# Splitting the two wide tiles of each attention diagonal into high and low parts, the low part made by VectorE

## The chip, the cores and the metric

The kernel runs on one core of a Trainium2 chip. Its time is in device microseconds (us). An execution gives one time; the profiled execution also gives the span from the first to the last instruction of the program.

## The reference, cut to what matters

The model is a feed-forward part (512 to 4096 to 512, 4-bit weights), causal attention, and the same feed-forward part again, each with a layer norm and a residual, on 2048 tokens of 512 features in fp32. The change is in attention:

```python
q, k, v = split(x_norm @ w_qkv.T + b_qkv)        # 16 heads of 32 features, 2048 tokens
scores = einsum('bhqd,bhkd->bhqk', q, k) / sqrt(32)
scores = scores + causal                          # -inf above the diagonal
out = einsum('bhqk,bhkd->bhqd', softmax(scores), v)
```

## The kernel before

Stages run one after the other: feed-forward, projections, `attention`, output projection, feed-forward. This change touches `attention` alone.

Within `attention` the queries of a head stand in 4 blocks of 512. Block b needs the key tiles 0 to 4b+3, 128 keys each, so a head has 4+8+12+16 = 40 tiles, called slots 0 to 39 here (`TILES`). In a block the key tiles 4b to 4b+3 lie on the diagonal and are 512, 384, 256 and 128 queries wide; all others are 512 wide. Block 0 has its diagonal tiles in slots 0, 1, 2, 3 (widest first). In the later blocks every b full tiles are followed by one diagonal tile, narrowest first, so the tiles of 384 and 512 queries stand in slots 9 and 11, 20 and 23, 35 and 39.

A product in full fp32 reads its operands as they are. A split product uses a high part (fp32r, rounded) and a low part (what the rounding left) and takes two matmuls in fp32r. Before the change the tiles below the diagonal (24 a head, `SPLIT`) have split probabilities, and the 16 diagonal tiles (`WHOLE`) plain fp32 ones.

Each engine works through its own instructions in the order written. For slot t they are:

- TensorE (PE), in `head`: the scores of slot t+4 (L1211, and L1215 for the mask on the diagonal), one chunk of scores of the next head for its row maxima (L699, L703), at slots 4, 12, 23 and 39 the "rows" (L712, four small transposes that bring the negated maxima of block 0, 1, 2 or 3 of the next head into the rows of its queries), then slot t's probabilities times the values: L1228 for a whole tile, L1231 and L1234 for high and low of a split one.
- ScalarE (ACT): the exponentials of slot t+4 from a score bank, L1283 for `probs`, and L1285 for `probs_high` of a split tile; rows back into `queries` (L742) at the slots of the rows; the block's output out of PSUM (L1292).
- GpSimd (POOL): `probs_low` = `probs` minus `probs_high` for the split tiles, one after the other (L1324).
- VectorE (DVE): the maximum of each chunk (L721). After the chunks of slots 2, 10, 21 and 37 it makes the block's maxima ready for the rows, with `split_max`: a reduction (L729), a CAST to fp32r (L734), and a subtraction of 4 columns (L736), the last of which lets the rows go.

What ties them: three score banks (the scores of slot t+4 wait for the exponentials of slot t+1), a ring of 5 slots for the probabilities, three banks for chunks and rows. The heads are 5 passes of a hardware loop over three heads, and the last head by itself, in which there is no next head, so no chunks, no maxima and no rows.

Of the kernel before, what the change touches and what calls it, by code (L numbers as in the profile page):

```python
# [16 lines left out]
P = 128  # L17
# [3 lines left out]
TB = 512  # L21
# [27 lines left out]
def f32(ap):  # L49

    return ap.bitcast(F32)
# [532 lines left out]
AHEAD = 4  # L584
RING = AHEAD + 1

WHOLE = [t for t in range(SLOTS) if TILES[t][1] >= 4 * TILES[t][0]]
SPLIT = [t for t in range(SLOTS) if t not in WHOLE]


def chunks_of_slot(t):

    return [m for m in range(SLOTS) if m * (SLOTS - 2) // SLOTS == t]
# [533 lines left out]
def attention(nc, bank, o_parts, sums, inverses, w_out, b_out, heads, o):  # L1127
    with ExitStack() as ctx:
# [3 lines left out]
        def sem(name):  # L1132
            return ctx.enter_context(nc.semaphore(name))
# [12 lines left out]
        scores_ready = sem("scores_ready")  # L1146
        probs_ready = sem("probs_ready")
        probs_low_ready = sem("probs_low_ready")
        out_ready = sem("out_ready")
        out_free = sem("out_free")  # L1150
        out_stored = [sem(f"out_stored{i}") for i in range(2)]
# [43 lines left out]
        @block.tensor  # L1195
        def _(pe):

            def scores(hp, s, t, first=False):

                b, kt = TILES[t]  # L1200
                i = s % 3
                if t in FIRST_OF_BLOCK:
                    pe.wait_ge(heads.rows_ready, 12 * hp + (4 * s + b + 1))
                    if s == 2 and b == 0:
                        pe.wait_ge(heads.constants_ready, 10)
                if not (first and t < SCORE_BANKS):
                    pe.wait_ge(probs_ready, 120 * hp + (SLOTS * s + t - SCORE_BANKS + 1))
                q0 = max(b * TB, kt * P)
                width = (b + 1) * TB - q0
                out = score_bank[(SLOTS * s + t) % SCORE_BANKS]  # L1210
                last = pe.matmul(out[:, 0:width], keys[i][0:ROWS, cols(kt, P)],  # L1211
                                 queries[i][0:ROWS, q0:q0 + width], start=True, stop=(kt < 4 * b),
                                 skip_group_check=True)
                if kt >= 4 * b:
                    last = pe.matmul(out[:, 0:P], heads.ident_b[:], heads.key_mask_b[:],  # L1215
                                     start=False, stop=True, skip_group_check=True)
                last.then_inc(scores_ready, 1)

            def with_values(hp, s, t):
                b, kt = TILES[t]  # L1220
                i = s % 3
                if t in FIRST_OF_BLOCK:
                    pe.wait_ge(out_free, 12 * hp + (4 * s + b + 1))
                pe.wait_ge(probs_ready, 120 * hp + (SLOTS * s + t + 1))
                off = max(0, kt * P - b * TB)
                out = out_bank[b % 2][0:VCOLS, off:TB]
                if t in WHOLE:
                    last = pe.matmul(out, f32(values[i][:, kt, :]), probs[:, t % RING, 0:TB - off],  # L1228
                                     start=(t in FIRST_OF_BLOCK), stop=(t in LAST_OF_BLOCK), skip_group_check=True)
                else:  # L1230
                    pe.matmul(out, values[i][:, kt, :], probs_high[:, t % RING, 0:TB - off],  # L1231
                              start=(t in FIRST_OF_BLOCK), stop=False, skip_group_check=True)
                    pe.wait_ge(probs_low_ready, 3 * len(SPLIT) * hp + (len(SPLIT) * s + SPLIT.index(t) + 1))
                    last = pe.matmul(out, values[i][:, kt, :], probs_low[:, t % RING, 0:TB - off],  # L1234
                                     start=False, stop=(t in LAST_OF_BLOCK), skip_group_check=True)
                if t in LAST_OF_BLOCK:
                    last.then_inc(out_ready, 1)

            def head(hp, s, has_next):
                for t in range(SLOTS):  # L1240
                    if t + AHEAD < SLOTS:
                        scores(hp, s, t + AHEAD)
                    elif has_next:
                        scores(hp, s + 1, t + AHEAD - SLOTS)
                    if has_next:
                        for m in chunks_of_slot(t):
                            heads.max_chunk(pe, hp, s + 1, m)
                        if t in ROWS_AT:
                            heads.rows(pe, hp, s + 1, ROWS_AT[t])
                    with_values(hp, s, t)  # L1250

            for t in range(AHEAD):
                scores(0, 0, t, first=True)
            with pe.Fori(0, HEADS // 3) as hp:
                for s in range(3):
                    head(hp, s, True)
            head(HEADS // 3, 0, False)

        @block.vector
        def _(dve):  # L1260
            def head(hp, s):
                for t in range(SLOTS):
                    for m in chunks_of_slot(t):
                        heads.take_max(dve, hp, s + 1, m)
                    if t in MAXED_AT:
                        heads.split_max(dve, hp, s + 1, MAXED_AT[t])

            heads.fill_ones(dve, 2)
            with dve.Fori(0, HEADS // 3) as hp:
                for s in range(3):  # L1270
                    head(hp, s)
            dve.wait_ge(o.sums_loaded, 16)
            early, _ = o.inverse_tile(EARLY_HEADS)
            dve.reciprocal(early, early).then_inc(o.inverse_ready, 1)

        @block.scalar
        def _(act):
            def exps(hp, s, t):
                b, kt = TILES[t]
                width = TB - max(0, kt * P - b * TB)  # L1280
                act.wait_ge(scores_ready, 120 * hp + (SLOTS * s + t + 1))
                source = score_bank[(SLOTS * s + t) % SCORE_BANKS][:, 0:width]
                last = act.activation(probs[:, t % RING, 0:width], source, ACT.Exp, scale=SM_SCALE)  # L1283
                if t in SPLIT:
                    last = act.activation(probs_high[:, t % RING, 0:width], source, ACT.Exp, scale=SM_SCALE)  # L1285
                last.then_inc(probs_ready, 1)

# [28 lines left out]
        @block.gpsimd  # L1316
        def _(pool):
            def low(hp, s, t):
                if t in WHOLE:
                    return  # L1320
                b, kt = TILES[t]
                width = TB - max(0, kt * P - b * TB)
                pool.wait_ge(probs_ready, 120 * hp + (SLOTS * s + t + 1))
                pool.tensor_tensor(probs_low[:, t % RING, 0:width], probs[:, t % RING, 0:width],  # L1324
                                   f32(probs_high[:, t % RING, 0:width]), ALU.subtract)\
                    .then_inc(probs_low_ready, 1)

            def head(hp, s):
                for t in range(SLOTS):
                    low(hp, s, t)  # L1330
# [235 lines left out]
```

## Time and profile before

| what | us |
|---|---|
| median of 3 runs (lowest, highest) | 3196.67 (3193.45, 3202.14) |
| the profiled execution: its time | 3196.54 |
| its span | 3194.7 |
| attention, from 1299 to 2008 us of the span | 709 |
| of it the last head | 40 |
| PE busy in those 709 us | 654.93 |
| ACT busy | 556.77 |
| POOL busy | 485.25 |
| DVE busy | 444.19 |

The busy time of PE is from modelled ends of pipelined matmuls, so the work of a matmul is better read from the distance between two starts. The times below are of one execution. The inner heads repeat: the same slot takes the same time in each but for a few hundredths of a us.

### The profile page before, as it was taken

The numbers are of one execution on the slowest core, as the hardware profiler recorded it, in microseconds if no ns is written. First come the engines' busy times: TensorE is split into PE (matmuls) and PEld (weight loads), VectorE is DVE, ScalarE is ACT, GpSimd is POOL, SyncE is SP. The second block draws the span as 40 slices with busy tenths as digits, with TensorE's granted clock in tenths as the row PEclk, the third lists the DMA queues.
The fourth block names the chain that finished last, engine by engine and source line by source line (L and its number), as shares of the span: only waits on it lengthen the run. The fifth ranks groups of instructions, "written<-read, shape, count | busy, mean of one in ns | idle before, by whom it ended". The sixth has DMA issues, their size and how long they took to land. (4 is left out here: it accounts for less than half of the span.)

```text
span 3194.7 us, 40306 instructions
## 1 busy us (share of the span) xinstructions
PE 3015.3 (94%) x13408; PEld 2316.5 (73%) x13408; DVE 1945.8 (61%) x2795; ACT 1263.3 (40%) x2213; POOL 1264.9 (40%) x880
## 2 busy tenths in 40 slices
PE   5999999999999989999999999669999999999999
PEld 3788888888888758555555555447888888888887
DVE  7666656665666465666666664476666566665664
ACT  4322222222222242677777778233222222222222
POOL 4322222222222175566666767433222222222221
PEclk9999999999999989999999999789999999999999
DMA  2000000000000039322222240310000000000001
GB/s 92 21 27 27 26 20 26 26 26 20 20 26 14 28 93 253 105 47 66 65 64 49 54 105 23 114 40 20 27 27 26 20 23 23 26 26 20 26 13 53
DMA packets 123898, 144.37 MB, mean 45 GB/s; under 512 B 71904, under 2 KB 72160, under 8 KB 120480
## 3 DMA queue, kind: packets, MB, share of 16 engines
q1 hardware_dynamic: 123256, 142.70, 15.8%
q8 instruction: 42, 0.69, 0.1%
q10 hardware_dynamic: 552, 0.59, 0.1%
q14 instruction: 48, 0.39, 0.0%
HBM read 105.26 MB, written 38.01 MB: 45 GB/s over the span
## 5 line engine op out<-in xcount | busy, mean ns | idle before, releaser
L60 PE MATMUL psum<-ffn_x_high,ffn_w_high 128*128 128x512 f32 x2048 | 803.3, 392 | 17.2 <-DVE ffn_gelu L388 17.2
L525 POOL TENSOR_TENSOR ffn_inner<-ffn_gelu,ffn_inner 128x512 fp32r<-128x512 f32 x256 | 346.2, 1352 | 1156.4 <-ACT ffn_inner L470 1156.4
L61 PE MATMUL psum<-ffn_x_low,ffn_w_high 128*128 128x512 f32 x2048 | 798.9, 390 | 0.0
L62 PE MATMUL psum<-ffn_x_high,ffn_w_low 128*128 128x512 f32 x2048 | 798.6, 390 | 0.0
L1324 POOL TENSOR_TENSOR probs_low<-probs,probs_high 128x512 fp32r<-128x512 f32 x384 | 483.5, 1282 | 223.7 <-ACT probs_high L1285 223.2
L378 DVE SCALAR_TENSOR_TENSOR ffn_gelu<-ffn_gelu,psum 128x512 f32<-128x512 f32 x256 | 176.0, 688 | 599.1 <-ACT ffn_gelu L463 599.0
L721 DVE TENSOR_REDUCE chunk_max<-psum 128x1 f32<-128x512 f32 (+3 forms) x640 | 383.4, 610 | 217.2 <-PE psum L699 113.0
L60 PEld LDWEIGHTS psum<-ffn_x_high,ffn_w_high 128*128 128x128 f32 x2048 | 386.2, 189 | 103.0 <-DVE ffn_gelu L388 20.9
L61 PEld LDWEIGHTS psum<-ffn_x_low,ffn_w_high 128*128 128x128 f32 x2048 | 386.0, 188 | 81.6 <-issue 2.0
L62 PEld LDWEIGHTS psum<-ffn_x_high,ffn_w_low 128*128 128x128 f32 x2048 | 385.7, 188 | 80.5
L60 PE MATMUL psum<-ffn_inner,ffn_w_high 128*128 128x512 f32 x1024 | 398.6, 389 | 0.2
L61 PE MATMUL psum<-ffn_inner,ffn_w_high 128*128 128x512 f32 x1024 | 398.4, 389 | 0.0
L62 PE MATMUL psum<-ffn_inner,ffn_w_low 128*128 128x512 f32 x1024 | 398.4, 389 | 0.0
L1283 ACT ACTIVATE probs<-psum 128x512 f32<-128x512 f32 (+3 forms) x640 | 341.4, 548 | 96.6 <-PE psum L1211 57.3
L463 ACT ACTIVATE ffn_gelu<-psum 128x512 f32<-128x512 f32 x256 | 152.8, 597 | 530.9 <-PE psum L62 530.9
L519 POOL TENSOR_TENSOR ffn_w_low<-ffn_weight,ffn_w_high 128x1024 fp32r<-128x1024 f32 x96 | 232.1, 2418 | 329.5 <-ACT ffn_w_high L456 329.5
L394 DVE SCALAR_TENSOR_TENSOR x<-psum,x 128x512 f32<-128x512 f32 x512 | 321.3, 683 | 16.0 <-PE psum L62 16.0
L470 ACT ACTIVATE ffn_inner<-ffn_gelu 128x512 fp32r<-128x512 f32 x256 | 161.9, 632 | 381.2 <-DVE ffn_gelu L388 381.2
L1211 PE MATMUL psum<-queries,keys 98*128 98x512 f32 (+3 forms) x640 | 298.5, 467 | 3.0 <-ACT probs_high L1285 2.1
L382 DVE SCALAR_TENSOR_TENSOR ffn_gelu<-ffn_gelu,psum 128x512 f32<-128x512 f32 x256 | 176.2, 688 | 180.0 <-ACT ffn_gelu L465 180.0
L456 ACT ACTIVATE ffn_w_high<-ffn_weight 128x1024 fp32r<-128x1024 f32 x96 | 102.0, 1062 | 398.9 <-DVE ffn_weight L369 398.9
L699 PE MATMUL psum<-keys,queries 96*128 96x512 f32 (+3 forms) x640 | 248.9, 398 | 1.0 <-DVE chunk_max L721 0.7
(124 smaller groups left out, 3989.3 us busy)
## 6 DMA issues: line engine op xcount, KB each, us to landing
ffn_words<-packed SPq DMA_DIRECT2D x96, 256.0 KB
ffn_word_scales<-scales SPq DMA_DIRECT2D x96, 256.0 KB
qk_parts<-parts SPq DMA_DIRECT2D x32, 512.0 KB, 4.4
queries<-qk_parts SPq DMA_DIRECT2D x48, 256.0 KB, 4.6
keys<-qk_parts SPq DMA_DIRECT2D x48, 256.0 KB, 6.6
v_parts<-parts SPq DMA_DIRECT2D x16, 512.0 KB, 6.1
values<-v_parts SPq DMA_DIRECT2D x16, 512.0 KB, 10.9
o_parts<-heads_out SPq DMA_DIRECT2D x64, 128.0 KB
```

Source lines behind the costliest of these rows:

```text
L60: pe.matmul(out, w_high, x_high, start=first, stop=False, skip_group_check=True)
L61: pe.matmul(out, w_high, x_low, start=False, stop=False, skip_group_check=True)
L62: return pe.matmul(out, w_low, x_high, start=False, stop=last, skip_group_check=True)
L382: dve.scalar_tensor_tensor(out=cubic[m], in0=square[m], scalar=1.0, in1=gate_bank[m], op0=ALU.add, op1=ALU.mult)\
L394: dve.scalar_tensor_tensor(out=x[:, k, cols(tb, TB)], in0=down_bank[k], scalar=FFN_BACK, in1=x[:, k, cols(tb, TB)], op0=ALU.mult, op1=ALU. ...
L519: pool.tensor_tensor(w_low[s][:, :, piece, :], weight[:, q % 2, :, :], f32(w_high[s][:, :, piece, :]), ALU.subtract).then_inc(w_low_ready, 1)
L525: pool.tensor_tensor(inner[:, tb % 2, m, 1, :], product[m], f32(inner[:, tb % 2, m, 0, :]), ALU.subtract)\
L699: last = pe.matmul(out[:, 0:width], self.queries[i][0:self.STACK, cols(qt, P)], self.keys[i][0:self.STACK, c * TB:c * TB + width], start=T ...
L721: dve.tensor_reduce(self.chunk_max[:, b % 2, qt % 4, c:c + 1], self.max_bank[max_bank_of(s, ("chunk", m))][:, 0:width], AX.X, ALU.max).the ...
L1211: last = pe.matmul(out[:, 0:width], keys[i][0:ROWS, cols(kt, P)], queries[i][0:ROWS, q0:q0 + width], start=True, stop=(kt < 4 * b), skip_g ...
L1283: last = act.activation(probs[:, t % RING, 0:width], source, ACT.Exp, scale=SM_SCALE)
L1324: pool.tensor_tensor(probs_low[:, t % RING, 0:width], probs[:, t % RING, 0:width], f32(probs_high[:, t % RING, 0:width]), ALU.subtract)\
```

## The change

The diagonal tiles of 512 and 384 queries (`WIDE`, 8 a head) get the same treatment as the tiles below the diagonal: ACT makes a second exponential into `probs_high`, PE makes two fp32r matmuls in place of one in fp32. Their low part is made by DVE, not by POOL, in `wide_low`, two slots ahead of the slot in which PE needs it, and has a semaphore of its own. The two narrow diagonal tiles (256 and 128 queries) stay plain fp32. POOL's list of work stays as it was. In the last head DVE, which had nothing to do there, gets the low parts of its wide tiles.

```diff
-WHOLE = [t for t in range(SLOTS) if TILES[t][1] >= 4 * TILES[t][0]]
-SPLIT = [t for t in range(SLOTS) if t not in WHOLE]
+WHOLE = [t for t in range(SLOTS) if TILES[t][1] >= 4 * TILES[t][0] + 2]
+WIDE = [t for t in range(SLOTS) if 0 <= TILES[t][1] - 4 * TILES[t][0] < 2]
+SPLIT = [t for t in range(SLOTS) if t not in WHOLE and t not in WIDE]
+WIDE_AHEAD = 2
...
-                    pe.wait_ge(probs_low_ready, 3 * len(SPLIT) * hp + (len(SPLIT) * s + SPLIT.index(t) + 1))
+                    if t in WIDE:
+                        pe.wait_ge(wide_low_ready, 3 * len(WIDE) * hp + (len(WIDE) * s + WIDE.index(t) + 1))
+                    else:
+                        pe.wait_ge(probs_low_ready, 3 * len(SPLIT) * hp + (len(SPLIT) * s + SPLIT.index(t) + 1))
...
+            def wide_low(hp, s, t):
+                if t not in WIDE:
+                    return
+                b, kt = TILES[t]
+                width = TB - (kt * P - b * TB)
+                dve.wait_ge(probs_ready, 120 * hp + (SLOTS * s + t + 1))
+                dve.tensor_tensor(probs_low[:, t % RING, 0:width], probs[:, t % RING, 0:width],
+                                  f32(probs_high[:, t % RING, 0:width]), ALU.subtract).then_inc(wide_low_ready, 1)
...
+            def head(hp, s, has_next):
                 for t in range(SLOTS):
-                    for m in chunks_of_slot(t):
-                        heads.take_max(dve, hp, s + 1, m)
-                    if t in MAXED_AT:
-                        heads.split_max(dve, hp, s + 1, MAXED_AT[t])
+                    if t + WIDE_AHEAD < SLOTS:
+                        wide_low(hp, s, t + WIDE_AHEAD)
+                    elif has_next:
+                        wide_low(hp, s + 1, t + WIDE_AHEAD - SLOTS)
+                    if has_next:
+                        for m in chunks_of_slot(t):
+                            heads.take_max(dve, hp, s + 1, m)
+                        if t in MAXED_AT:
+                            heads.split_max(dve, hp, s + 1, MAXED_AT[t])
...
-                if t in SPLIT:
+                if t not in WHOLE:
                     last = act.activation(probs_high[:, t % RING, 0:width], source, ACT.Exp, scale=SM_SCALE)
...
             def low(hp, s, t):
-                if t in WHOLE:
+                if t not in SPLIT:
                     return
```

DVE's queue of the kernel before, around slot 21 of a head: the chunk maxima (TENSOR_REDUCE of `chunk_max`) of slots 20 and 21, and the maxima of block 2 made ready for the rows.

```order
L721 TENSOR_REDUCE chunk_max<-psum 128x1
L719 REGISTER_ALU
L721 TENSOR_REDUCE chunk_max<-psum 128x1
L729 TENSOR_REDUCE minus_max<-chunk_max 128x4
L731 REGISTER_ALU
L733 REGISTER_ALU
L734 CAST max_parts<-minus_max 128x4
```

The same place of DVE's queue after the change, where the lines of the code stand three further down:

```order
L724 TENSOR_REDUCE chunk_max<-psum 128x1
L1273 REGISTER_ALU
L1274 TENSOR_TENSOR probs_low<-probs,probs_high 128x512
L722 REGISTER_ALU
L724 TENSOR_REDUCE chunk_max<-psum 128x1
L732 TENSOR_REDUCE minus_max<-chunk_max 128x4
L734 REGISTER_ALU
L736 REGISTER_ALU
L737 CAST max_parts<-minus_max 128x4
```

The low part of slot 23 (512 queries) now stands between the maximum of slot 20's chunk and that of slot 21's, ahead of the three steps that the rows of block 2 wait for. At slot 37 the low part of slot 39 stands in the same way ahead of block 3's, and the low parts of slots 9 and 11 ahead of the maxima of slots 7 and 9.

PE's queue before, around slot 23: a chunk of the next head, the rows of block 2, slot 23's product with the values, and the scores of slot 28.

```order
L699 MATMUL psum<-keys,queries 128x512
L709 REGISTER_ALU
L686 REGISTER_ALU
L712 MATMUL psum<-ident_r,max_parts 2x128 x4
L1228 MATMUL psum<-probs,values 65x512
L1207 REGISTER_ALU
L1211 MATMUL psum<-queries,keys 128x512
```

PE's queue after, at the same place:

```order
L702 MATMUL psum<-keys,queries 128x512
L712 REGISTER_ALU
L689 REGISTER_ALU
L715 MATMUL psum<-ident_r,max_parts 2x128 x4
L1235 MATMUL psum<-probs_high,values 65x512
L1238 REGISTER_ALU
L1241 MATMUL psum<-probs_low,values 65x512
L1211 REGISTER_ALU
L1215 MATMUL psum<-queries,keys 128x512
```

Nothing of PE's order has moved: two matmuls stand where one stood, and between them is a wait for DVE.

## Rows read from the trace of the kernel before

**Rows 1.** Windows of attention; busy us and instructions of each engine, clock, DMA.

```profile
1299.00:2008.00 709.00, 654.93 (x3256) 402.87 (x3256) 444.19 (x783) 556.77 (x1150) 485.25 (x387) 0.98 0.26 62
```

**Rows 2.** Waits in attention: who waited for whom, total us, times, longest.

```profile
PE psum L712 <- DVE max_parts L736: 48.6, 45, 1.9
```

**Rows 3.** Timeline of PE, slots 10 to 12: start us, us, what, [idle before].

```profile
1538.05 0.40 PE L1211 MATMUL psum<-queries,keys 98*128 98x512 f32 x1
1538.28 0.40 PE L699 MATMUL psum<-keys,queries 96*128 96x512 f32 x1
1538.51 1.02 PE L1228 MATMUL psum<-probs,values 128*65 128x512 f32 x2
...
1539.61 0.39 PE L699 MATMUL psum<-keys,queries 96*128 96x512 f32 x1
```

**Rows 4.** Timeline of ACT, slots 19 to 21, then two of its pauses before.

```profile
1543.72 0.61 ACT L1285 ACTIVATE probs_high<-psum 128x512 fp32r<-128x512 f32 x1
1544.20 0.99 ACT L1283 ACTIVATE probs<-psum 128x384 f32<-128x384 f32 x2
1545.05 0.63 ACT L1285 ACTIVATE probs_high<-psum 128x512 fp32r<-128x512 f32 x1
...
1535.46 0.60 ACT L1283 ACTIVATE probs<-psum 128x512 f32<-128x512 f32 x1 [0.33 <-PE psum L1211]
1538.48 0.60 ACT L1283 ACTIVATE probs<-psum 128x512 f32<-128x512 f32 x1 [0.78 <-PE psum L1211]
```

**Rows 5.** Timeline of DVE and POOL in the output projection: both read SBUF.

```profile
2014.21 0.69 DVE L1424 TENSOR_TENSOR from_high<-from_high,from_low 128x512 f32<-128x512 f32 x1 [41.95 <-PEq L1128]
2016.37 3.40 POOL L1474 TENSOR_TENSOR normed_low<-from_high,normed_high 128x512 fp32r<-128x512 f32 x2 [5.61 <-ACT normed_high L1467]
2016.88 1.76 DVE L1424 TENSOR_TENSOR from_high<-from_high,from_low 128x512 f32<-128x512 f32 x1
```

**Rows 6.** Timeline of DVE and POOL around the rows of block 1.

```profile
1538.79 0.37 DVE L734 CAST max_parts<-minus_max 128x4 fp32r<-128x4 f32 x1
...
1536.62 2.51 POOL L1324 TENSOR_TENSOR probs_low<-probs,probs_high 128x512 fp32r<-128x512 f32 x2 [0.62 <-ACT probs_high L1285]
1539.64 2.62 POOL L1324 TENSOR_TENSOR probs_low<-probs,probs_high 128x512 fp32r<-128x512 f32 x2 [0.50 <-ACT probs_high L1285]
```

**Rows 7.** Timeline of all engines around the rows of block 2.

```profile
1548.75 3.75 POOL L1324 TENSOR_TENSOR probs_low<-probs,probs_high 128x512 fp32r<-128x512 f32 x3 [0.28 <-ACT probs_high L1285]
...
1546.59 1.93 DVE L721 TENSOR_REDUCE chunk_max<-psum 128x1 f32<-128x384 f32 x3 [0.38 <-PE psum L703]
1549.01 0.69 DVE L721 TENSOR_REDUCE chunk_max<-psum 128x1 f32<-128x512 f32 x1 [0.49 <-PE psum L703]
...
1550.03 1.28 DVE L734 CAST max_parts<-minus_max 128x4 fp32r<-128x4 f32 x1
...
1551.34 1.18 DVE L736 TENSOR_TENSOR max_parts<-minus_max,max_parts 128x4 fp32r<-128x4 f32 x1
...
1552.65 0.40 PE L712 MATMUL psum<-ident_r,max_parts 128*2 128x128 f32 x4 [1.86 <-DVE max_parts L736]
```

**Rows 8.** Timelines of POOL, DVE and PE around the rows of block 3.

```profile
1561.76 5.02 POOL L1324 TENSOR_TENSOR probs_low<-probs,probs_high 128x512 fp32r<-128x512 f32 x4
...
1566.77 0.69 DVE L721 TENSOR_REDUCE chunk_max<-psum 128x1 f32<-128x512 f32 x1 [0.38 <-PE psum L703]
...
1568.28 0.40 PE L712 MATMUL psum<-ident_r,max_parts 128*2 128x128 f32 x4 [0.27 <-DVE max_parts L736]
```

**Rows 9.** Timeline of POOL in the last head.

```profile
1981.40 24.89 POOL L1324 TENSOR_TENSOR probs_low<-probs,probs_high 128x512 fp32r<-128x512 f32 x20 [0.17 <-ACT probs_high L1285]
```

**Rows 10.** Timelines behind a loop's turn, and a window (columns as in rows 1).

```profile
1572.15 0.60 ACT L1283 ACTIVATE probs<-psum 128x512 f32<-128x512 f32 x1 [1.98 <-PE psum L1215]
1575.96 0.59 PE L712 MATMUL psum<-ident_r,max_parts 128*2 128x128 f32 x4 [1.34 <-DVE max_parts L736]
...
1575.00:1582.00 7.00, 6.04 (x27) 4.01 (x28) 3.88 (x7) 4.68 (x10) 3.32 (x3) 0.76 1.10 217
```

More of the change, by code:

```diff
@@ L1148, in attention @@
         probs_low_ready = sem("probs_low_ready")
+        wide_low_ready = sem("wide_low_ready")
         out_ready = sem("out_ready")
@@ L1260, in _ @@
         def _(dve):
-            def head(hp, s):
-                for t in range(SLOTS):
-                    for m in chunks_of_slot(t):
-                        heads.take_max(dve, hp, s + 1, m)
-                    if t in MAXED_AT:
-                        heads.split_max(dve, hp, s + 1, MAXED_AT[t])
+            def wide_low(hp, s, t):
[7 more added lines that the diff above has]
+            def head(hp, s, has_next):
+                for t in range(SLOTS):
+                    if t + WIDE_AHEAD < SLOTS:
[7 more added lines that the diff above has]
+                            heads.split_max(dve, hp, s + 1, MAXED_AT[t])
             heads.fill_ones(dve, 2)
+            for t in range(WIDE_AHEAD):
+                wide_low(0, 0, t)
             with dve.Fori(0, HEADS // 3) as hp:
                 for s in range(3):
-                    head(hp, s)
+                    head(hp, s, True)
             dve.wait_ge(o.sums_loaded, 16)
@@ L1274, in _ @@
             dve.reciprocal(early, early).then_inc(o.inverse_ready, 1)
+            head(HEADS // 3, 0, False)
         @block.scalar
```

## The prediction

> **What bounds the kernel now.** The windows say where to look: in attention PE is busy 654.93 of 709 us, ACT 557, POOL 485, DVE 444 [rows 1]. PE sets the pace. What it loses goes mostly to one wait, the rows' wait for DVE's last step of the maxima: 48.6 us in 45 waits, of 60 rows, four a head in 15 heads [rows 2]. The timelines say why. The rows of block 2 idle 1.86 us and those of block 3 0.27 us [rows 7, 8]; 48.6 over 15 heads is 3.24 a head, so 1.1 are left for block 0, if those of block 1 (the fourth that 45 of 60 leaves out) have none.
>
> DVE's CAST on 4 columns takes 0.37 us at one place and 1.28 at another [rows 6, 7], and at 1550.03 to 1552.52 both the CAST and the subtraction end just where two of POOL's three subtractions end (1548.75 plus 1.25 for each gives 1550.00, 1551.25 and 1552.50). So DVE's instructions that take two operands or two ports from SBUF wait while POOL runs, and POOL takes over again between the CAST and the subtraction. With large tiles the two alternate: a subtraction of 512 columns is 0.69 us alone, and 1.76 us when it starts 0.5 us into POOL's; POOL's two took 3.40 us, not 2.5 [rows 5]. I read the 0.9 as two waits, for a DVE instruction that ran when POOL came and for the one at 2016.88 that got in between. So a DVE low part costs DVE 0.60 us between neighbours and the POOL instruction behind it 0.44 us, 384 columns three quarters of that.
>
> **PE's part.** The fp32 product of 512 columns: from its start at 1538.51 to the next L699 at 1539.61 is 1.10 us; of that 0.23 is the one scores' matmul between them (as from 1538.05 to 1538.28), so it costs 0.87 us. Two fp32r ones cost 0.46. Saved: 0.40. At 384 columns three quarters: 0.29 [rows 3]. Four of each a head are 2.76 us, over 15 heads 41.4 us. This is the gain if nothing else moves.
>
> **ACT's part.** A second exponential is 0.48 us at 512 columns (1543.72 to 1544.20), and 0.37 at 384 (0.85 for a 384 and a 512, from 1544.20 to 1545.05) [rows 4]. That is 3.4 us a head; with 16 heads ACT goes from 557 to 611 us and stays below PE. Where it stands ahead of a due slot it eats pauses: between slots 9 and 15 it gets 0.85 us more work and had pauses of 0.33 and 0.78 us [rows 4]. It just fits.
>
> **The rows, one after the other.** Here the gain is kept or lost, so I carry the sum through a head. Times are those of before plus the shift.
>
> Block 0 (slot 4). PE is 0.69 us earlier (slots 0, 1). Slot 2's maximum and the exponential that POOL's next subtraction waits for both hang on PE, so all move together and the wait of 1.1 us stays [rows 2]. Shift -0.69.
>
> Block 1 (slot 12). Slots 9 and 11 bring PE there 1.38 us early, at 1538.46 (0.23 behind the last row of [rows 3] is 1539.84). DVE reaches its CAST 0.98 us earlier, as slot 9's saving counts there but not slot 11's, at 1537.81 [rows 6]. POOL does not follow: its pair began at 1536.62, behind ACT. ACT's added 0.85 us leave slot 12's high part 0.3 us earlier, not 0.98, so POOL's pair starts at 1536.31 and goes to 1538.83. Then slot 15's subtraction is ready (its exponential moves by 0.98 with its scores, from 1538.48 to 1537.50, and the second ends 1.08 later, at 1538.58) and follows at once. The CAST is held to 1538.86 and the small subtraction, free before, is held until 1540.10. The rows go at 1540.23: a new wait of 1.77 us. Shift -1.38 + 1.77 = +0.39.
>
> Block 2 (slot 23). Slot 20 saves 0.29: +0.10. `wide_low` of slot 23 stands ahead of the last chunk's maximum. Its probabilities are there by 1547.9: ACT reaches slot 21's second exponential at 1545.05 plus 0.37 for slot 20, and has then four of 0.48, the last complete 0.60 after its start [rows 4]. DVE's chunks before it ended at 1548.52, now some 0.35 later, so it is free at 1548.85, and POOL pauses there (0.28 us before 1548.75) [rows 7], now until 1549.1, as slot 24's exponentials move with PE, by up to 0.39. DVE gets in first, to 1549.43; POOL's next subtraction ends at 1550.6. The maximum of the last chunk, taken at 1549.01 before, is taken at 1549.45, the CAST comes 1.02 us behind its start as before, at 1550.46, waits 0.15 us and not 0.95, and the small subtraction waits for one whole subtraction of POOL, to 1551.87. The rows go at 1552.0, not 1552.65. The wait falls from 1.86 to 1.11 us. Shift +0.10 - 0.75 = -0.65, and -1.05 behind slot 23's product.
>
> Block 3 (slot 39). POOL is nearly the bound here: four subtractions without a pause end at 1566.78 [rows 8]. Slot 35's low part costs it 0.33 us. Shifted, its last one runs from 1564.8 to 1566.05. DVE comes to slot 39's low part at 1565.0, ahead of the last chunk's maximum, and is held to 1566.05, done at 1566.58. The maximum (0.69) and the three small steps unhindered (0.82, as from 1567.46 to 1568.28 before) bring the rows to 1568.0. PE was ready at 1568.01 (1568.28 less 0.27), is now at 1566.67 (1.05 + 0.29 earlier), and waits 1.33 us. Shift -0.28, and -0.66 behind slot 39's product, rounded.
>
> **The sum.** The low parts of slots 0 and 1 come when DVE has no chunk. So a head gives -2.76 + 1.77 - 0.75 + 1.06, that is -0.66 us: 15 heads -9.9. In the four heads behind a turn of the loop ACT idles 1.98 us, and DVE's CAST meets POOL's first subtraction; there PE waits 1.34 us [rows 10]. DVE comes 0.69 earlier and passes before POOL starts: 0.65 us more each, -2.6. The last head is bound by POOL: 20 subtractions without a pause in 24.89 us [rows 9]. Four low parts get between them (two of 0.44, two of 0.33), ACT's 0.85 ahead of them delay their start, and the last product saves 0.40: +2.0. Together -10.5 us. The profiled execution took 3196.54 (its span 3194.7), 0.1 from the median, so the forecast is 3186.0.
>
> **The clock.** After the wait at 1575.96 the granted clock is 0.76 over 7 us [rows 10], so TensorE went part of the time at 1.2 of its 2.4 GHz, behind the idle time. That is 1.7 us lost (0.24 of 7). In attention the clock is 0.98 [rows 1], so 709 times 0.02, some 14 us, of such stretches. The change removes four such waits and adds others (slots 12, 39). I take no change; bounds are 7 us either way.
>
> **A page that speaks against it.** The Trainium skill (SBUF — State Buffer, "SBUF: two separate sides") says that VectorE and GpSimd share a port pair under an exclusive lock, held for the whole instruction, and that a VectorE instruction with two SBUF inputs needs it. The trace agrees: 1.76 us beside 0.69 [rows 5]. By that rule the times of the two engines add up on the pair. In numbers of this case: POOL's 485 us and 64 low parts, half of 0.60 and half of 0.45 us (67 us), are 552 of some 700 us. So the pair is no bound on the average, and what it costs is where one instruction stands behind another, as in the walk above.
>
> **Rivals.**
>
> A. The waits stay as they are, and all of PE's 41.4 us show, less the last head's 2.0: 3157. For it: DVE is idle 265 of 709 us. Against it: the walk above puts four low parts into POOL's way. Chance 0.10.
>
> B. Slower: DVE comes too late to slot 23's low part, after POOL has begun slot 24's. The margin is 0.25 us (1548.85 against 1549.1); and it rests on times that I carried over twenty slots. Then the low part ends at 1550.95, and the last maximum, CAST and small subtraction follow with two more subtractions of POOL between: rows at 1553.5, 1.5 us later than forecast, in 15 heads +22: 3208. It decides as soon as DVE is 0.25 us later there, for then DVE waits for the whole of POOL's instruction. Chance 0.22.
>
> C. The small subtraction at block 1 slips in before POOL. It needs slot 15's high part 0.25 us later than 1538.58, or POOL's pair earlier by as much; then one subtraction less, 1.25 us in 15 heads, -19: 3167. Chance 0.20.
>
> D. Nothing moves, because what PE saves, each row gives back: 3197. Chance 0.05.
>
> The forecast itself has 0.43. Its own bounds: a clock of 7 us either way, and 0.3 us a head for the price of POOL's delay (0.3 to 0.7 us a low part): 3176 to 3198.
>
> **The numbers.** Under A and C it is faster; so is the forecast in some 45 of 100 of its cases, since 0.3%, what a measurement of this kernel tells from no change, is 9.6 us and the forecast stands at 10.5. Faster 0.49, same 0.28, slower 0.23. The range leaves A out below and the upper half of B above: 3163 to 3210.
>
> **What the profile of the changed kernel would show.** PE's two matmuls for slot 23 0.46 us, no fp32 product of 512 columns left. Four rows a head with waits of 1.1, 1.8, 1.1, 1.3 us: the wait of PE for DVE's last small step grows from 48.6 us to about 73. DVE's low parts of 0.6 us where POOL rests and 1.0 to 1.8 where it doesn't. In the last head POOL's 20 subtractions end about 2.4 us later. If the rows of block 1 go without a wait, C holds; if those of block 2 wait about 2.8 us, B does. The prediction is wrong if ACT turns out to hold PE back (its waits for exponentials are short now), or if POOL and DVE don't take turns as in the output projection.

## The result: slower, 3227.1 us against 3197.0

| | before | changed |
|---|---|---|
| median, us | 3197.01 (6 runs, 3192.85 to 3202.14) | 3227.06 (6 runs, 3200.16 to 3234.43) |
| ratio | 1 | 1.0075, 95% interval 1.0044 to 1.0105 |
| profiled execution, us (span) | 3196.54 (3194.7) | 3202.68 (3200.9) |

The forecast was 3186.0, its range 3163 to 3210. The six times of the changed kernel fall into two groups: 3200.16 and 3202.68, and four from 3225.72 to 3234.43. The profile is of the run of 3202.68, one of the two low ones, so what it shows is the smaller part of the loss; the first experiment shows the larger. "DVE's low part" below is the subtraction that DVE makes for a wide tile (line 1274).

The page of the changed kernel, two lines of it, and the window of its attention (columns as in [rows 1]):

```profile
span 3200.9 us, 40712 instructions
...
PE 2974.4 (93%) x13408; PEld 2315.1 (72%) x13408; DVE 2055.4 (64%) x2923; ACT 1306.0 (41%) x2341; POOL 1274.5 (40%) x880
```
```profile
1299.00:2014.00 715.00, 618.10 (x3260) 403.04 (x3260) 553.70 (x914) 600.59 (x1279) 497.19 (x388) 0.97 0.26 62
```

PE's busy time in attention fell from 654.93 us [rows 1] to 618.10, as the change means it to. DVE's rose by 109.5 us where the forecast's low parts were 67. From its first scores to its last product attention takes 708.7 us before and 711.3 after. That is 2.6 of the 6.2 us by which the two spans differ; the other 3.6 fall outside attention (2.2 ahead of it, 1.4 behind it), where the code is the same, and are taken as spread between executions.

The waits in attention (who waited for whom, total us, times, longest) answer to [rows 2]:

```profile
PE psum L715 <- DVE max_parts L739: 73.5, 56, 2.2
...
PE psum L1241 <- DVE probs_low L1274: 12.9, 3, 7.6
```

The first line is the rows' wait, 48.6 us before, and "about 73" was forecast. The second was not forecast: three times PE waited for a low part of DVE's.

**What went as forecast.** The timelines of PE, then of DVE and POOL, around the rows of block 1 (line 715 is the old 712, 1235 and 1241 multiply the high and the low part, 737 is the CAST, 739 the small subtraction):

```profile
1630.96 0.39 PE L1235 MATMUL psum<-probs_high,values 128*65 128x512 f32 x1
1631.18 0.39 PE L1241 MATMUL psum<-probs_low,values 128*65 128x512 f32 x1
...
1633.63 0.40 PE L715 MATMUL psum<-ident_r,max_parts 128*2 128x128 f32 x4 [1.57 <-DVE max_parts L739]
```
```profile
1631.23 1.06 DVE L737 CAST max_parts<-minus_max 128x4 fp32r<-128x4 f32 x1
1632.32 1.18 DVE L739 TENSOR_TENSOR max_parts<-minus_max,max_parts 128x4 fp32r<-128x4 f32 x1
...
1629.72 5.00 POOL L1348 TENSOR_TENSOR probs_low<-probs,probs_high 128x512 fp32r<-128x512 f32 x4 [0.65 <-ACT probs_high L1309]
```

The second product starts 0.23 us behind the first, and the next matmul 0.23 behind the second (0.46 together, where the prediction reads 0.87 from [rows 3] for the fp32 one). The CAST, 0.37 us in [rows 6], takes 1.06, the small subtraction 1.18: POOL's four subtractions now stand together, and both steps of DVE's end where one of them ends (near 1632.3 and 1633.5). The rows wait 1.57 where they had waited for nothing. Blocks 2 and 3 of the same head:

```profile
1642.27 0.68 DVE L1274 TENSOR_TENSOR probs_low<-probs,probs_high 128x512 fp32r<-128x512 f32 x1
...
1643.87 0.26 DVE L737 CAST max_parts<-minus_max 128x4 fp32r<-128x4 f32 x1
1644.16 1.18 DVE L739 TENSOR_TENSOR max_parts<-minus_max,max_parts 128x4 fp32r<-128x4 f32 x1
...
1645.47 0.40 PE L715 MATMUL psum<-ident_r,max_parts 128*2 128x128 f32 x4 [1.14 <-DVE max_parts L739]
...
1654.62 1.29 DVE L1274 TENSOR_TENSOR probs_low<-probs,probs_high 128x384 fp32r<-128x384 f32 x1
...
1658.53 1.57 DVE L1274 TENSOR_TENSOR probs_low<-probs,probs_high 128x512 fp32r<-128x512 f32 x1
...
1661.53 0.40 PE L715 MATMUL psum<-ident_r,max_parts 128*2 128x128 f32 x4 [1.32 <-DVE max_parts L739]
```

Slot 23's low part comes in a pause of POOL's of 0.46 us (and takes 0.68 us) and the rows of block 2 wait 1.14, not the 1.86 of [rows 7]. Slot 35's takes 1.29 and slot 39's 1.57, each behind one subtraction of POOL, and the rows of block 3 wait 1.32, not the 0.27 of [rows 8].

**What did not.** DVE, POOL and PE at slot 35 in the first head, and then DVE at slot 35 in the second head:

```profile
1340.89 0.69 DVE L724 TENSOR_REDUCE chunk_max<-psum 128x1 f32<-128x512 f32 x1 [0.21 <-PE psum L702]
1341.49 5.04 DVE L1274 TENSOR_TENSOR probs_low<-probs,probs_high 128x384 fp32r<-128x384 f32 x1
1346.46 2.53 DVE L724 TENSOR_REDUCE chunk_max<-psum 128x1 f32<-128x384 f32 x4
...
1337.39 8.73 POOL L1348 TENSOR_TENSOR probs_low<-probs,probs_high 128x512 fp32r<-128x512 f32 x7
...
1343.64 0.34 PE L1235 MATMUL psum<-probs_high,values 128*65 128x384 f32 x1
1346.59 0.58 PE L1241 MATMUL psum<-probs_low,values 128*65 128x384 f32 x1 [2.62 <-DVE probs_low L1274]
```
```profile
1387.22 0.69 DVE L724 TENSOR_REDUCE chunk_max<-psum 128x1 f32<-128x512 f32 x1 [0.22 <-PE psum L702]
1387.83 1.29 DVE L1274 TENSOR_TENSOR probs_low<-probs,probs_high 128x384 fp32r<-128x384 f32 x1
```

The same instruction with the same neighbours takes 5.04 us in one head and 1.29 in the next. The row of POOL's shows the last seven of eight subtractions without a pause (from 1336.15 on). The seven take 8.73 us, 1.247 each, so no DVE instruction got between any of them: they change at 1342.38, 1343.63 and 1344.87, all while DVE waits, and end at 1346.12. DVE is done at 1346.53, 0.41 us after POOL stopped of itself: behind slot 35 it had slots 36, 37 and 38 to do, and the next ones are DVE's (39) or on the next head's diagonal. This is called a miss from here on: DVE did not get in at a change of POOL's instruction, and then not at the next ones either. PE waited 2.62 us for it. The last head, DVE, POOL and PE:

```profile
1997.78 11.20 DVE L1274 TENSOR_TENSOR probs_low<-probs,probs_high 128x384 fp32r<-128x384 f32 x2 [9.06 <-ACT probs_high L1309]
...
1996.03 7.47 POOL L1348 TENSOR_TENSOR probs_low<-probs,probs_high 128x512 fp32r<-128x512 f32 x6
2003.43 4.52 POOL L1365 TENSOR_TENSOR wo_low<-wo,wo_high 128x2048 fp32r<-128x2048 f32 x1
...
2008.42 0.58 PE L1241 MATMUL psum<-probs_low,values 128*65 128x384 f32 x1 [7.63 <-DVE probs_low L1274]
```

Here DVE asks at 1997.78 and is let in at 2007.95, when `wo_low`, whose work has nothing to do with this head, is through as well. (POOL's row shows the last six of 20 subtractions without a pause.) All 128 low parts together (the view of one line: duration in ns, least, median, most):

```profile
L1274 DVE TENSOR_TENSOR probs_low<-probs,probs_high x128: 546/684/10596, 1303.5 to 2008.3; 128x512 fp32r<-128x512 f32 x64, 128x384 fp32r<-128x384 f32 x64
```

Only three of them are above 1.7 us, all of slot 35: 5.04 and 5.03 in the first and third head and 10.60 in the last.

### The profile page after: what moved, and what is told of

It reads as the page before. It is cut to its first block and busy times, and to the rows that moved or that the text cites. A ratio compares the mean times of both kernels' runs of the same rounds, so it can differ in the third digit from the quotient of the medians.

```text
span 3200.9 us, 40712 instructions
## 1 busy us (share of the span) xinstructions
PE 2974.4 (93%) x13408; PEld 2315.1 (72%) x13408; DVE 2055.4 (64%) x2923; ACT 1306.0 (41%) x2341; POOL 1274.5 (40%) x880
## 5 line engine op out<-in xcount | busy, mean ns | idle before, releaser
L1348 POOL TENSOR_TENSOR probs_low<-probs,probs_high 128x512 fp32r<-128x512 f32 x384 | 492.6, 1307 | 209.7 <-ACT probs_high L1309 208.7
L1307 ACT ACTIVATE probs<-psum 128x512 f32<-128x512 f32 (+3 forms) x640 | 361.6, 573 | 39.1 <-PE psum L1215 20.4
L1309 ACT ACTIVATE probs_high<-psum 128x512 fp32r<-128x512 f32 (+1 forms) x512 | 324.5, 634 | 0.0
L1215 PE MATMUL psum<-queries,keys 98*128 98x512 f32 (+3 forms) x640 | 254.9, 399 | 7.1 <-ACT probs_high L1309 6.2
```

## The experiments

In each, the ratio is to the kernel before, run beside it on the same chip: its median was 3195.09 for experiments 1 to 4, 3194.54 for 5 to 8 and 3194.97 for 9 and 10. The theory under test: what the change costs beyond the forecast is misses at slot 35. The rivals: it costs what the new waits of the rows cost, or POOL's being slowed, or ACT's added exponentials.

**1. The changed kernel again.** No edit, for a second profile.

> The changed kernel once more, for its spread and for a second profile. Theory S (starving): DVE's low part of slot 35 comes while POOL's subtractions follow one another without a pause, and gets in either at the first change between two of them or at none until POOL rests; each miss makes PE wait some 3 us, 8 us in the last head. Then the times fall in two groups, about 3200 and 3225 to 3235 us, and the slower a profile is, the more of slot 35's 16 low parts take 5 us or more (3 of 16 in the first profile; about 10 in a run of 3228). Theory C (clock): the slower executions have the same 3 misses and more stretches at 1.2 GHz behind the waits of the rows.

Measured: 3233.86 (3225.95 to 3234.84), ratio 1.0115 (1.0099 to 1.0130). The profile is of a run of 3233.04, one of the high group. Its waits and its low parts:

```profile
PE psum L715 <- DVE max_parts L739: 62.8, 49, 2.2
...
PE psum L1241 <- DVE probs_low L1274: 39.2, 13, 7.6
```
```profile
1431.45 5.07 DVE L1274 TENSOR_TENSOR probs_low<-probs,probs_high 128x384 fp32r<-128x384 f32 x1
```

13 of 16 low parts of slot 35 missed (twelve of 4.97 to 5.07 us, 10.60 in the last head) where the other profile has 3. The spans are 3231.2 and 3200.9, so 10 misses more go with 30.3 us more: 3.0 us each. They can be taken apart. PE waits 26.3 us more for line 1274 and 10.7 less for the rows (behind a miss the rows of block 3 mostly find their maxima ready); that is 15.6. The other half goes with the clock. The window of attention (columns as in [rows 1]):

```profile
1299.00:2045.00 746.00, 632.58 (x3260) 408.16 (x3260) 579.06 (x913) 603.32 (x1279) 493.44 (x388) 0.95 0.25 59
```

PE is busy 632.58 us with the same 3260 matmuls that took it 618.10 in the other profile, 14.5 more, and the granted clock is 0.95 against 0.97. Where the clock falls, two windows of the first profile's missed first head show:

```profile
1341.00:1346.00 5.00, 2.98 (x15) 1.63 (x13) 5.00 (x2) 3.83 (x8) 5.00 (x5) 1.00 0.00 0
1346.00:1350.00 4.00, 3.41 (x11) 1.88 (x11) 3.49 (x6) 1.48 (x4) 0.12 (x1) 0.57 0.00 0
```

PE is busy 2.98 of 5 us, and right behind that the granted clock is 0.57, most of the time the 1.2 GHz level. Not every miss is followed by this: behind the one at 1431.45 in the second profile the clock stays at 1.00. In these two profiles, then, the kernel's two speeds are few misses and nearly always a miss; the other eight runs of it have no profile.

**2. Slot 35 stays plain fp32.**

```diff
-WHOLE = [t for t in range(SLOTS) if TILES[t][1] >= 4 * TILES[t][0] + 2]
-WIDE = [t for t in range(SLOTS) if 0 <= TILES[t][1] - 4 * TILES[t][0] < 2]
+WIDE = [0, 1, 9, 11, 20, 23, 39]
+WHOLE = [t for t in range(SLOTS) if TILES[t][1] >= 4 * TILES[t][0] and t not in WIDE]
```

> Slot 35 (384 queries, block 3) stays plain fp32, the seven other wide tiles are split as in the change. Theory S: no low part meets four POOL subtractions in a row in the middle of block 3, no run is slow: all within 6 us, median 3185 to 3192 (the last head's wait of 8 us and those of 3 us gone, 0.29 us a head of PE's gain lost). Theory C: the waits of the rows stay and with them the clock's stretches, so the times still spread to 3225 and more.

Measured: 3183.21 (3181.14 to 3185.85), ratio 0.9966 (0.9952 to 0.9979), 2 us below the expected range. Without this one low part of eight the change is 12 us faster than before, and 50.7 us faster than with it (experiment 1); the rows' waits at blocks 1 and 2 are still there. One miss is left, in the last head, at slot 39 (6.76 us):

```profile
L1274 DVE TENSOR_TENSOR probs_low<-probs,probs_high x112: 549/683/6758, 1299.9 to 1983.0; 128x512 fp32r<-128x512 f32 x64, 128x384 fp32r<-128x384 f32 x48
```

**3. No low part by DVE at all.**

```diff
-                    if t in WIDE:
-                        pe.wait_ge(wide_low_ready, 3 * len(WIDE) * hp + (len(WIDE) * s + WIDE.index(t) + 1))
-                    else:
+                    if t not in WIDE:
                         pe.wait_ge(probs_low_ready, 3 * len(SPLIT) * hp + (len(SPLIT) * s + SPLIT.index(t) + 1))
-                    last = pe.matmul(out, values[i][:, kt, :], probs_low[:, t % RING, 0:TB - off],
+                    second = probs_high if t in WIDE else probs_low
+                    last = pe.matmul(out, values[i][:, kt, :], second[:, t % RING, 0:TB - off],
...
             def wide_low(hp, s, t):
-                if t not in WIDE:
-                    return
+                return
```

> The low part of the wide tiles is left out: DVE makes none, and PE's second matmul for such a tile reads the high part again, so PE and ACT have the work of the change and DVE and POOL that of before. Theory S, and the walk of the prediction: PE's 41 us show nearly whole, as the rows wait about as before: 3155 to 3168. Rival theory A (ACT's added exponentials hold PE back, not the port): 3185 or more.

This kernel leaves the low parts of the wide tiles out: PE's second product takes the high part once more, so its numbers are not the model's, and only its time is of use.

Measured: 3154.56 (3152.13 to 3156.65), ratio 0.9870 (0.9855 to 0.9886), 0.4 us below the expected range. ACT still makes its 128 added exponentials and PE its two products each, so ACT is not what makes the changed kernel slow. It also takes the rows' waits apart: 1.01, 1.6, 0.93 and 0.28 us at blocks 0 to 3 (0 and 0.99 at blocks 0 and 1 behind a loop's turn).

```profile
PE psum L715 <- DVE max_parts L739: 52.7, 57, 1.8
```

Block 1's new wait of 1.6 us comes without any low part of DVE's, from PE's earlier arrival and POOL's later pair, as the forecast derived it. Block 3's is the low parts' (0.28 without them).

**4. Low parts at slots 0, 1, 20 and 23 alone** (`WIDE = [0, 1, 20, 23]`, WHOLE as in 2).

> Only slots 0, 1, 20 and 23 of a head are split with DVE's low part; 9, 11, 35 and 39 stay plain fp32. By the walk of the prediction slots 9 and 11 bring a wait of 1.6 us ahead of the rows of block 1 for 0.69 us of PE, and 35 and 39 one of 1.0 us for as much; without them a head gives 0.69 + 0.29 + 0.40 and 0.7 us less wait at the rows of block 2, about 2.1 us: 3165, within 3160 to 3175, without slow runs. Theory C expects no better than 3190.

Measured: 3157.77 (3156.30 to 3158.71), ratio 0.9882 (0.9867 to 0.9897), below the expected range. The rows of block 1 don't wait, those of block 2 wait 1.35 us, those of block 3 0.28. A head takes 41.72 us instead of 43.6: twice 0.69 saved, 0.5 less wait at block 2, 1.88 together. That is 28 us in 15 heads. The rest goes with the clock: in the kernel before, seven of the 14 periods from one head's rows of block 2 to the next have a granted clock of 0.96 and are 1.5 to 2.5 us longer than 43.6, 14 us together, and here all 14 have 1.00. Four of the eight tiles bring nearly all that can be had.

**5. Slot 35 alone** (`WIDE = [35]`).

> Slot 35 alone is split with DVE's low part; the other seven stay plain fp32 as before. Theory S: PE gains 0.29 us a head (-4 us in all), each of the 16 low parts takes either 1.3 us or, when it is missed at every change of POOL, about 5; each miss costs 3 us, that of the last head 7. So 3198 us if only the last is missed, about 3240 if nearly all are. A rival theory, that the cost comes from the eight low parts together (DVE's load), expects 3190 to 3196 and no low part over 2 us.

Measured: 3225.19 (3217.18 to 3233.33), ratio 1.0105 (1.0086 to 1.0124). It lies within the expected 3198 to 3240. A single low part a head makes the kernel about as slow as all eight do.

```profile
L1274 DVE TENSOR_TENSOR probs_low<-probs,probs_high x16: 767/1293/10510, 1341.1 to 2012.0; 128x384 fp32r<-128x384 f32 x16
```

The profiled run is the lowest of its four (3217.18) and has four misses (4.7, 5.05, 5.05 and 10.51 us). Its attention is 18.9 us longer than that of before. In the kernel with this one tile a head without a miss takes 43.3 us at a clock of 1.00, 0.3 less than before, -4 us in 14 periods; the three periods with a miss are 5.1, 3.9 and 4.0 us above 43.3, with a clock of 0.93 and twice 0.96; and from the last rows of block 2 to the end it takes 9.6 us more. That adds up to 18.4; the periods at a low clock without a miss cost about as much as before (15 and 14 us).

**6. The changed kernel, and POOL made to yield once.** POOL waits, before its subtraction of slot 36, until slot 35's low part is done:

```diff
+                if t == 36:
+                    pool.wait_ge(wide_low_ready, 3 * len(WIDE) * hp + (len(WIDE) * s + WIDE.index(35) + 1))
```

> The changed kernel with one wait more: POOL starts slot 36's subtraction only when DVE's low part of slot 35 is done, so DVE gets the port at the latest there. The work is the same. Theory S: no low part of slot 35 over about 2 us, the last head's neither, the two groups of times become one: 3184 to 3192. The rival, that POOL must not be held up in block 3, expects each head longer by the wait: 3205 or more.

Measured: 3181.87 (3178.89 to 3185.16), ratio 0.9959 (0.9946 to 0.9973). All of the computation of the changed kernel is here, one wait is added, and the time is 45 us under the changed kernel's median (and 2 us below the expected range).

```profile
L1274 DVE TENSOR_TENSOR probs_low<-probs,probs_high x128: 549/684/2439, 1301.8 to 1987.4; 128x512 fp32r<-128x512 f32 x64, 128x384 fp32r<-128x384 f32 x64
```
```profile
1299.00:1992.00 693.00, 609.89 (x3256) 395.32 (x3256) 536.29 (x911) 598.52 (x1279) 493.66 (x388) 0.99 0.27 64
```

No low part is above 2.44 us, PE waits for none, and attention takes 692.3 us at a clock of 0.99. In all 15 inner heads POOL pauses 0.50 us ahead of slot 36, and DVE takes 1.29 to 1.35 us. The 2.44 us are of the last head: there DVE was passed over at one change of POOL's, and got in at the next, where POOL waits for it:

```profile
1983.38 2.44 DVE L1274 TENSOR_TENSOR probs_low<-probs,probs_high 128x384 fp32r<-128x384 f32 x1 [9.07 <-ACT probs_high L1309]
...
1973.83 11.58 POOL L1350 TENSOR_TENSOR probs_low<-probs,probs_high 128x512 fp32r<-128x512 f32 x9
1985.97 4.19 POOL L1350 TENSOR_TENSOR probs_low<-probs,probs_high 128x512 fp32r<-128x512 f32 x3 [0.56 <-DVE probs_low L1274]
```

The rows still wait (1.0, 1.6, 1.14 and, two heads of three, 1.34 us: 68.0 us in 51), so these waits are not what made the kernel slow. With experiments 2 and 5 this settles the cause.

**7. The maxima before the low part.** In each slot DVE first takes its chunk's maximum and the small steps and then makes the low part of the slot two ahead:

```diff
-                    if t + WIDE_AHEAD < SLOTS:
-                        wide_low(hp, s, t + WIDE_AHEAD)
...
                         if t in MAXED_AT:
                             heads.split_max(dve, hp, s + 1, MAXED_AT[t])
+                    if t + WIDE_AHEAD < SLOTS:
+                        wide_low(hp, s, t + WIDE_AHEAD)
```

> In DVE's order of each slot the chunk maxima and the steps for the rows come first and the low part two slots ahead comes behind them. By the walk of the prediction the rows of block 3 wait 0.3 us and not 1.3, and PE waits 0.1 to 0.4 us for slot 39's low part in its place; the wait of block 1's rows (1.6 us) stays, as it comes from ACT and POOL. Slot 35's low part still meets POOL without a pause, so misses of 5 us are still there and set the time: 3190 with few, 3225 with many. If the low parts' place ahead of the maxima were the cause of the loss, the time would be 3180 without any change at slot 35.

Measured: 3238.97 (3232.78 to 3245.42), ratio 1.0137 (1.0118 to 1.0155), 14 us above the 3225 expected with many misses.

```profile
PE psum L715 <- DVE max_parts L739: 52.0, 48, 2.2
...
PE psum L1241 <- DVE probs_low L1274: 41.8, 15, 7.6
```

The rows of block 3 wait 0.3 us or nothing, so the rival "the rows' waits" would have this faster. Instead it is slower than the changed kernel: slot 35's low part, asked for about 1 us later, takes 4.0 to 4.1 us in 14 of 15 heads and 10.6 in the last. Asking later makes a held low part shorter by as much and does not prevent the miss. The granted clock of attention is 0.94 here.

**8. Slots 9 and 11 alone** (`WIDE = [9, 11]`).

> Slots 9 and 11 alone are split with DVE's low part. By the walk of the prediction PE gains 0.69 us a head ahead of the rows of block 1, ACT's two added exponentials keep POOL where it was, and the rows wait 1.6 to 1.8 us in place of none: 0.9 us a head longer, so 3205 to 3212 us. If the gain of PE were kept there, 3185.

Measured: 3215.39 (3209.82 to 3219.05), ratio 1.0060 (1.0044 to 1.0075), 3 us above the expected range.

```profile
PE psum L715 <- DVE max_parts L739: 74.2, 61, 1.9
```

There are no misses (no low part above 0.91 us). The rows of block 1 wait 1.54 to 1.62 us in all 15 heads, and a head takes 44.7 us instead of 43.6: 0.69 saved and 1.58 lost is 0.9 of these 1.1. This pair is a loss by itself, which the sum of the forecast contained (-0.69 + 1.77 for these slots) and hid among gains.

**9. The version that follows:** slots 0, 1, 20, 23 and 35, with the wait of experiment 6. Slots 9, 11 and 39 stay plain, because their rows give back what they save: for 9 and 11 experiment 8 shows it; slot 39 was not run alone, but in experiment 2 the rows of block 3 wait 0.71 to 0.79 us instead of 0.28, for 0.40 saved behind them.

```diff
+WIDE = [0, 1, 20, 23, 35]
+WHOLE = [t for t in range(SLOTS) if TILES[t][1] >= 4 * TILES[t][0] and t not in WIDE]
...
+                if t == 36:
+                    pool.wait_ge(wide_low_ready, 3 * len(WIDE) * hp + (len(WIDE) * s + WIDE.index(35) + 1))
```

> Slots 0, 1, 20, 23 and 35 split with DVE's low part, and POOL's subtraction of slot 36 waits for slot 35's low part; 9, 11 and 39 stay plain fp32. If the accounts of the earlier runs add up, this is the kernel with slots 0, 1, 20, 23 (3157.8 us) less up to 0.29 us in 15 heads, so 3153 to 3157, with no low part over 2.5 us. If the handover costs POOL more than PE gains in block 3, it is 3160 or more.

Measured: 3151.24 (3150.15 to 3152.73), ratio 0.9861 (0.9844 to 0.9877): 44 us faster than before, 76 faster than the changed kernel, and 2 us below the expected range.

```profile
PE psum L715 <- DVE max_parts L739: 31.4, 26, 1.4
```
```profile
L1274 DVE TENSOR_TENSOR probs_low<-probs,probs_high x80: 549/768/2419, 1301.8 to 1956.1; 128x384 fp32r<-128x384 f32 x48, 128x512 fp32r<-128x512 f32 x32
```

**10. POOL makes the wide low parts too** (`WIDE = []` and every tile that isn't whole in SPLIT), DVE none.

> All eight wide tiles split as in the change, but POOL makes their low parts too, in the order of slots, and DVE has the work of before. Then nobody is missed at the port, but POOL gets about 8 us a head more (four of 1.25, four of 0.95) on 30, and in block 3 17.2 us for a stretch of 16: PE waits for POOL there. Theory S expects 3195 to 3215 without two groups of times. If the low parts' engine did not matter, it would be 3187, as the forecast.

Measured: 3286.86 (3284.92 to 3293.58), ratio 1.0290 (1.0273 to 1.0307), some 70 us above the expected range.

```profile
L738 DVE CAST max_parts<-minus_max x60: 357/2148/4217, 1306.2 to 2051.1; 128x4 fp32r<-128x4 f32 x60
```
```profile
PE psum L716 <- DVE max_parts L740: 130.1, 60, 3.8
```

I had priced only POOL's time. With fewer rests on POOL, DVE's CAST on 4 columns, never above 1.28 us before, takes 4.2 us at block 2 and 3.1 at block 3 in every head, and PE waits 3.7 and 3.1 us for it. These are misses as well, of another DVE instruction: at block 2 three changes of POOL's pass while the CAST waits, at block 3 two, and it is done only when POOL stops. So it is neither the low part's size nor its line that makes them. The granted clock of attention falls to 0.90.

## Why the prediction was wrong

**PE's part** (-2.76 us a head) was right: 0.46 for two products, and PE's busy time fell by 37 us.

**The rows** were right, block by block: waits of 1.01, 1.6, 1.14 and 1.33 us against 1.1, 1.77, 1.11 and 1.33. From the rows of block 2 to those of the next head a head without a miss or a stretch at a low clock takes 42.9 us after and 43.6 before: -0.66 forecast (the terms written down add up to -0.68), -0.66 to -0.7 measured. Behind a loop's turn two errors cancel, which is luck: the rows of block 0 wait 0 or 0.12 us instead of 1.34 [rows 10], a gain of 1.2 to 1.3 where 0.65 was forecast, and the rows of block 1 wait 2.05 to 2.21 us there instead of 1.6, which gives 0.5 to 0.6 of it back.

**The step that failed** is the price of DVE's low part: "With large tiles the two alternate", read from one instruction of [rows 5] and taken over to block 3 ("Slot 35's low part costs it 0.33 us") and to the last head ("Four low parts get between them"). It holds for most of the 128. At slot 35 DVE asks in the middle of eight or nine subtractions of POOL without a pause (20 in the last head), and may not get in until they end: 5.0 us instead of 1.3, 10.6 in the last head, 3.0 us of the kernel's time for each miss. The text itself named this as what would make it wrong ("if POOL and DVE don't take turns as in the output projection") and gave it neither a price nor a chance. A price was in reach. [rows 8] shows only the end of POOL's stretch at block 3, four subtractions in 5.02 us; the trace of the kernel before has eight without a pause, 10.00 us:

```profile
1556.78 10.00 POOL L1324 TENSOR_TENSOR probs_low<-probs,probs_high 128x512 fp32r<-128x512 f32 x8 [0.15 <-ACT probs_high L1285]
```

In the last head it has 24.89 us [rows 9], and `wo_low`'s 4.51 us follow at once. A DVE instruction that gets in only at the end of a stretch waits that long at most. Behind slot 35 three subtractions are left, so a miss holds the low part some 3.7 us longer, up to 56 us in 15 heads (an estimate from 1.25 us each). That bound would have put the range's top well above 3210.

**Rival B** had the right sign and its 3208 is near the lower group, but that is luck, as its mechanism did not occur: at slot 23 DVE was in time in all 15 heads (0.68 us). **Rival A** fell, as the rows' waits did change. **Rival C** fell: the small subtraction of block 1 took 1.18 us in all 15 heads, 0.16 before. **Rival D** fell: where nothing is missed (experiment 6) the rows don't give back all that PE saves.

**The clock** was put at 0, 7 us either way, and is more. Where nothing is missed it gains: in experiment 6 attention is 16.4 us shorter than before, and the forecast has -10.5. The undisturbed heads there take 43.10 us on the mean and give 0.5 each, 7 in all. Of the 14 periods from one head's rows of block 2 to the next, seven were longer by 1.5 to 2.5 us before, at a granted clock of 0.96 where the others have 1.00. Four of these seven were the ones with a loop's turn, where the forecast named the low clock and took no change. With the wait two are longer, by 1.4 and 1.6. That is the other 11 of the 18 us that the periods give back. The first and last head cost 1.9, where +2.0 was forecast. With misses the clock loses instead: it is about half of the 3.0 us of each.

**The sum.** What the forecast described is a kernel without misses. The nearest to it that was run is the one with the wait: 3181.87, against 3186.0. Its heads give less than forecast (0.5, not 0.66) and its clock more (11 us, not 0), so part of this agreement is luck.

A slip in the text: it speaks of "64 low parts, half of 0.60 and half of 0.45 us (67 us)". There are 128, 64 of each; the 67 us are right. The Trainium skill (SBUF — State Buffer, "SBUF: two separate sides") says that the engine that starts first holds the pair for its whole instruction and the other is fully blocked. The traces agree (1.29 us for 384 columns beside 0.55 at slots 9 and 1). What decided this case is another question: who comes next when POOL has its next instruction ready. The traces show both outcomes, 1.29 and 5.04 us for the same instruction.

**What stays open:** what decides a miss. Between the two profiles of the same kernel ten heads changed from let in to missed, and none the other way, and the two kinds of heads look alike: POOL's subtractions start 1.24 to 1.26 us apart and DVE asks 0.8 to 0.9 us ahead of POOL's change in both. The records don't resolve it. That the loss at a miss is split between wait and clock is worked out from windows, not tested by itself. Why heads without a miss run at a lower clock in some periods and not in others is open too (experiment 8 has no miss and 0.97).

## What to carry to other kernels

Before work is given to DVE with both operands in SBUF, look at what POOL does at that moment. Where POOL rests, the work costs its own time; where POOL stands in a stretch without a pause, price it as waiting to the end of that stretch, and either leave that tile alone or make POOL wait for it once (here one semaphore wait was worth 45 us). Look at the whole stretch for that, not at the rows of a narrow window. And take such a change tile by tile: a saving on PE that is followed by rows which wait for another engine is a loss (slots 9 and 11: +0.6%), and the five tiles that are left of eight bring 1.4% where all eight cost 0.75%.

## What the runs showed of the hardware

- A DVE instruction with two SBUF operands that asks during back-to-back POOL subtractions of 1.25 us is let in at the first change (1.29 to 1.35 us for 384 columns, 0.55 alone) or passed over at each change until POOL stops: 3 changes (5.0 us), or five and a 4.52 us instruction (10.6 us). In the two profiles of the changed kernel no low part lies between 1.7 and 4.9 us.
- The same holds for a CAST on 4 columns: 4.2 us at block 2 in all 15 heads of experiment 10, 0.17 undisturbed.
- One kernel spread over 34 us from run to run (3200.16 to 3234.43), with 3 misses in a run of 3203 and 13 in one of 3233; the kernel before stays within 14 (3190.28 to 3203.70), and without slot 35's low part or with POOL's wait it is 5 and 6.
- The granted clock of attention went with PE's waits, not with misses alone: 0.99 in experiments 2, 4, 6 and 9, 0.98 before, 0.97 with 3 misses and also with none in experiment 8 (rows waiting 74 us), 0.95 with 13, 0.90 with the rows waiting 130 us.
